# A mixed shared and routed FFN: the combination of a pair of tiles divided over two places of VectorE's step, and the first rows and last stores moved

## The chip, the cores and the metric

The kernel runs on one core of a Trainium2 chip. The metric is the device time of one execution in microseconds; the median of the runs is compared. The engines are TensorE (PE: matmul and transpose through the array), VectorE (DVE), ScalarE (ACT), GpSimd (POOL) and SyncE (SP), which here issues nearly all transfers. Each engine runs its own instruction stream in order, and they meet only through semaphores.

## What is computed

x is [4, 1024, 512] in float32: 4096 rows, 32 tiles of 128 rows. The reference is one modulated block: a time mix and channel mix, then a feed-forward with one shared and eight routed experts. Only the last part touches the change:

```
x = x + ga * attn(layernorm(x) * (1 + ca) + sa)
h = layernorm(x) * (1 + cb) + sb
shared = silu(h @ Wsg.T) * (h @ Wsu.T) @ Wsd.T                 # 704 wide
routed = sum over the two best experts of  w_e * (silu(h @ Wg_e.T) * (h @ Wu_e.T)) @ Wd_e.T   # 352 wide
x = x + gb * (routed + shared)
```

Products are made in three matmuls each: every float32 factor is split into a rounded high part and the remainder (names ending in _hi and _lo), and high x high, high x low and low x high are summed.

## The kernel before

The kernel has stages. After the time mix and the channel mix (stages one and two, up to about 900 us) come three sweeps over the feed-forward: EARLY (tiles 0 to 15 through the shared expert), ROUTED (39 expert tiles of 256 rows, 78 units of 128) and LATE (tiles 16 to 31 through the shared expert). The shared expert is 704 wide and is done as two halves of 352; one (tile, half) is a unit, and its work is the same as that of a routed unit.

A unit is a fixed chain. TensorE makes the up products into PS_G and PS_U (24 matmuls of 352 columns, lines 449 to 451), ScalarE makes silu (L1060), VectorE multiplies into hid (L1537), TensorE turns hid (L1815), ScalarE copies the high part out (hid_hi, L1053), VectorE subtracts for hid_lo (L1541), and TensorE makes the down product (nine matmuls of 512 columns, L1839 to L1841). The two halves of a tile add up in one bank, PS_Y. After half 1 VectorE gates the bank by mod3 and adds it to the residual rows in `base` (base_of, L1549 and L1554). TensorE works one unit ahead: in a step it turns hid of the unit before, makes the up product of this unit, then the down product of the unit before. The order within a step is written by hand, in `late_step` of each engine (L771 for SP, L1143 for ScalarE, L1634 for VectorE, L1887 for TensorE), and `sweep_part` unrolls the first and last steps around a hardware loop. t counts tiles: LATE's steps run from 15 to 32.

```
# TensorE, one late step (L1893 to L1899)
if t.back(-1).real(): turn_shared(LATE, t.back(-1))
for half in range(2):
    turn_hid(*before); up(LATE, t, half); down(*before)
```

`down` of half 0 also waits until VectorE has gated the previous tile's bank (L1829).

Beside the units, the late sweep combines the routed results. GpSimd gathers, for each pair of tiles q, the rows of the best and the second best expert (cb_y1, cb_y2, L908). ScalarE makes cb_out = w1 * cb_y1 (`first_product`, L1130 to L1141); VectorE adds w2 * cb_y2 (L1623, 'both'), multiplies by the gate (L1628, 'gated') and adds `base` (L1631, 'out'); SP stores the pair's 512 KB (`store_out`, L765). One pair is combined in each step: q = t - 17 on ScalarE and VectorE (steps 17 to 32), q = t - 18 on SP. ScalarE does first_product(q) and VectorE combine(q) at the very end of the step, after both halves. The buffers cb_y1, cb_y2 and cb_out have two slots, and lie in the two raw buffers that held unsplit weights before. The profile calls all three raw.

SP's lines that are touched: `load_late_rows` (L740) loads the 128 rows of a late tile into ex_x once the slot's former rows are turned; `load_shared_again` (L748) loads one half of the shared weights (2 MB) once the raw buffer is free; `routed_step` (L754) calls the latter in its last two steps, and the first late rows are loaded only after both, by the late sweep (L771). The wait at the end (L780) is for all stores.

Of the kernel before, what the change touches and what calls it, by code (L numbers as in the profile page):

```python
# [12 lines left out]
ALU = mybir.AluOpType  # L13
# [6 lines left out]
P = 128  # L20
D = 512
C = D // P
B, T = 4, 1024
N = B * T
NT = N // P
TPB = T // P
# [7 lines left out]
NJ = (2 * N + E * (R - 1)) // R  # L34
NU = NJ * R // P
SPLIT = NT // 2
# [78 lines left out]
LATE = Part(SPLIT, NT, NU, NU, ROUTED)  # L115
# [32 lines left out]
def build(nc, io, out):  # L148
    x_d = io["x"].rearrange("b t d -> (b t) d")
    out_d = out.rearrange("b t d -> (b t) d")  # L150
# [9 lines left out]
    h3_d = scratch("h3_rows", [N, D])  # L160
# [4 lines left out]
    with ctx:  # L165
# [143 lines left out]
        base = sb("base", [P, NT, D])  # L309
# [5 lines left out]
        w2 = sb("w2", [P, NT, 1])  # L315
# [211 lines left out]
        def _(sp):  # L527
# [209 lines left out]
                    sp.wait_ge(*x_pe.done(SPLIT + 2 * t.n + half - 2, "turned"))  # L737
                    sp.dma_start(ex_x[:, half, :], xs_d[bass.ds(row_of, P), :]).then_inc(ex_in[half], 16)

            def load_late_rows(t):  # L740
                row_of = sp.snap(t.n * P) if t.pair is not None else t.n * P
                sp.wait_ge(*x_pe.done(t.n + NU - 2, "turned"))
                sp.dma_start(ex_x[:, t.p, :], h3_d[bass.ds(row_of, P), :]).then_inc(sx_in[t.p], 16)

            for k in range(SC):
                sp.wait_ge(sc_out[k], 32 * len(range(k, NT, SC)))

            def load_shared_again(i):  # L748

                t = Tile(None, NJ + i, NJ + 2)  # L750
                sp.wait_ge(*rw_lo_vec.done(t.n - 2, "dn_lo"))
                load_raw(sp, t.p, io["sh_gu"][i], io["sh_dn"][i])

            def routed_step(t):  # L754
                if t.back(-1).real():
                    load_rows(t.back(-1))
                if t.real() and t.back(-2).real():
                    load_expert(t.back(-2))
                if t.pair is None and t.n in (NJ - 2, NJ - 1):
                    load_shared_again(t.n - (NJ - 2))  # L760

            sweep(sp, NJ, 2, 0, routed_step)
# [7 lines left out]

            def late_step(t):  # L771
                if t.back(-2).real():
                    load_late_rows(t.back(-2))
                    load_residual(t.back(-2))
                q = t.pairs_since(SPLIT + 2)
                if q.real():
                    store_out(q)

            sweep_part(sp, LATE, 2, 2, late_step)
            for p in range(2):  # L780
                sp.wait_ge(final_out[p], 16 * (NT // 4))
            sp.wait_ge(zero_out, 16 * NT)


# [129 lines left out]
        def _(act):  # L914
# [167 lines left out]
            def store_y(t, half):  # L1082
                row_of = act.snap((2 * t.n + half) * P) if t.pair is not None else (2 * t.n + half) * P
                act.wait_ge(*y_row_vec.done(2 * t.n + half, "y"))
                act.dma_start(ys_d[bass.ds(row_of, P), :], y_rows[:, half, :]).then_inc(ys_out[half], 16)
# [44 lines left out]
            def first_product(t):  # L1130

                if t.back(2).real():
                    act.wait_ge(final_out[t.p], 16 * t.half)
                else:
                    act.wait_ge(*rw_lo_vec.done(NJ + 1, "dn_lo"))
                act.wait_ge(y1_in[t.p], 32 * t.half + 32)
                act.activation(act_col[:, t.p:t.p + 1], eps[:], ACT.Copy)
                for a in range(2):
                    last = act.activation(cb_out[:, t.p, a, :], cb_y1[:, t.p, a, :], ACT.Copy,
                                          scale=w1[:, bass.ds(2 * t.n + a, 1), :].rearrange("p a b -> p (a b)"))  # L1140
                last.then_inc(cb_act.sem, 1)  # L1141

            def late_step(t):  # L1143
                q = t.pairs_since(SPLIT + 1)
                if t.real():
                    if t.back(-1).real():
                        shared_x_hi(LATE, t.back(-1))
                    for half in range(2):
                        if t.only(SPLIT):
                            expert_hi(Tile(None, NJ + 1, NJ + 2), half)  # L1150
                        hidhi(*LATE.before(t, half))
                        silu(LATE, t, half)
                        if t.only(SPLIT):
                            store_y(ROUTED.last(), half)
                elif t.only(NT):
                    hidhi(LATE, LATE.last(), 1)
                if q.real():
                    first_product(q)

            sweep_part(act, LATE, 1, 1, late_step)  # L1160

# [2 lines left out]
        def _(dve):  # L1164
# [374 lines left out]
            def hidlo(part, t, half):  # L1539
                dve.wait_ge(*u_act.done(part.unit(t, half), "hid_hi"))  # L1540
                dve.tensor_tensor(flat(hid_lo[:]), PS_H[:, 0:FK * P], flat(hid_hi[:]).bitcast(F32),  # L1541
                                  ALU.subtract).then_inc(u_vec.sem_of["hid_lo"], 1)
# [72 lines left out]
            sweep_part(dve, ROUTED, 1, 1, routed_step)  # L1615


            def combine(t):
                batch = t.n // (TPB // 2)
                dve.wait_ge(y2_in[t.p], 32 * t.half + 32)  # L1620
                dve.wait_ge(*cb_act.done(t.n, "first"))
                for a in range(2):
                    last = dve.scalar_tensor_tensor(cb_out[:, t.p, a, :], cb_y2[:, t.p, a, :],  # L1623
                                                    w2[:, bass.ds(2 * t.n + a, 1), :].rearrange("p a b -> p (a b)"),
                                                    cb_out[:, t.p, a, :], ALU.mult, ALU.add)
                last.then_inc(cb_vec.sem, 1)
                dve.wait_ge(*cb_vec.done(t.n, "both"))
                dve.tensor_tensor(cb_out[:, t.p], cb_out[:, t.p], mod3[:, bass.ds(batch, 1), :].to_broadcast([P, 2, D]),  # L1628
                                  ALU.mult).then_inc(cb_vec.sem, 1)
                dve.wait_ge(*cb_vec.done(t.n, "gated"))  # L1630
                dve.tensor_tensor(cb_out[:, t.p], cb_out[:, t.p], base[:, bass.ds(2 * t.n, 2), :],  # L1631
                                  ALU.add).then_inc(cb_vec.sem, 1)

            def late_step(t):  # L1634
                q = t.pairs_since(SPLIT + 1)
                if t.real():
                    if t.back(-1).real():
                        x_lo(t.back(-1).p, t.back(-1).n + NU)
                    for half in range(2):
                        before = LATE.before(t, half)  # L1640
                        hidlo(*before)
                        hid_of(LATE, t, half)
                        if t.only(SPLIT):
                            expert_lo(Tile(None, NJ + 1, NJ + 2), half)
                        if before[0] is ROUTED:
                            y_of_unit(*before[1:])
                        elif not half:
                            base_of(LATE, t.back(1))
                elif t.only(NT):
                    hidlo(LATE, LATE.last(), 1)  # L1650
                    base_of(LATE, LATE.last())
                if q.real():
                    combine(q)

            sweep_part(dve, LATE, 1, 1, late_step)

# [284 lines left out]
```

## Time and profile before

| what | us |
|---|---|
| median of 3 runs | 1899.61 (1895.79 to 1904.87) |
| profiled execution | 1899.84 |
| its span, first to last instruction | 1898.1 |
| late sweep, from its first turn to the last store | about 1647 to 1898 |

| engine | busy us | share |
|---|---|---|
| TensorE | 1753.4 | 92% |
| VectorE | 1331.3 | 70% |
| ScalarE | 722.7 | 38% |
| GpSimd | 567.6 | 30% |

A span is what lies between the first and the last instruction; the execution's time has 1.7 us around it. In the timeline a row is one instruction (or several alike), with its start, its duration, and in brackets the idle time of the engine just before it and what ended that. In the chain that ended last a row says how much a piece adds to it, which for overlapping matmuls is less than their duration. The granted clock is a share of TensorE's full 2.4 GHz; at 0.5 it is 1.2.

### The profile page before, as it was taken

What the parts mean: (1) busy time and instruction counts of PE and PEld (TensorE: products, weight loads), DVE (VectorE), ACT (ScalarE), POOL (GpSimd) and SP (SyncE); (2) the same over time, 40 slices, a digit from 0 to 9 for tenths busy, and PEclk for the clock granted to TensorE, in tenths of its full rate; (3) what the DMA queues carried; (4) which work ended last, traced back from release to release, by engine and by line L of the source; (5) the groups of instructions that cost most, each with busy time, mean ns of one, the idle gap of its engine ahead of it and who ended that gap; (6) DMA issues with size and microseconds to landing.
All of it is one profiled execution on the core that took longest, in us unless ns stands there. A gap on an engine that the chain in (4) does not pass through costs nothing.

```text
span 1898.1 us, 30073 instructions
## 1 busy us (share of the span) xinstructions
PE 1753.4 (92%) x9188; PEld 1520.5 (80%) x9188; DVE 1331.3 (70%) x2365; ACT 722.7 (38%) x1150; POOL 567.6 (30%) x659
## 2 busy tenths in 40 slices
PE   4599999997888999987899999999999999999997
PEld 0488888885777777776889989999999999888886
DVE  4899999983899888896733246666666666655555
ACT  2344444442444343343211135454545454422222
POOL 0343333322577667664125500000000000033432
PEclk8699999999998888897999999999999999999998
DMA  8333334334844433433167626767676767645442
GB/s 331 102 116 120 120 120 120 120 98 135 304 148 135 149 136 134 140 99 103 56 233 257 232 69 221 249 230 252 227 255 225 250 234 244 222 141 159 139 159 89
DMA packets 143262, 326.23 MB, mean 172 GB/s; under 512 B 20280, under 2 KB 20280, under 8 KB 137712
## 3 DMA queue, kind: packets, MB, share of 16 engines
q1 hardware_dynamic: 121744, 271.65, 42.9%
q0 software_dynamic: 10240, 33.56, 5.4%
q10 hardware_dynamic: 11232, 20.45, 2.8%
q8 instruction: 23, 0.38, 0.1%
q14 instruction: 23, 0.19, 0.0%
HBM read 217.56 MB, written 108.05 MB: 172 GB/s over the span
## 4 chain that ended last, share of the span: by engine, by line
PE 70%; DVE 18%; issue 5%; DMA 3%; ACT 2%; another core or an unknown queue 1%; DVEq 1%; POOL 1%; SPq 0%; ACTq 0%; POOLq 0%
PE bank L449 17%; PE bank L451 16%; PE bank L450 16%; DVE mix L1340 5%; PE bank L1839 5%; PE bank L1841 4%; PE bank L1840 4%; PE bank L460 4%; PE bank L1815 2%; DVE xh L1325 2%; DVE raw L1628 1%; DMA ex_x<-h_rows 1%; DMA stage<-in_w_k 1%; DVE h_lo L1395 1%; DVE raw L1623 1%
## 5 line engine op out<-in xcount | busy, mean ns | idle before, releaser
L449 PE MATMUL bank<-gu_hi,ex_x_hi 128*128 128x352 f32 x1136 | 382.4, 337 | 2.3 <-DVE gu_lo L1560 1.5
L451 PE MATMUL bank<-gu_hi,ex_x_lo 128*128 128x352 f32 x1136 | 369.6, 325 | 0.0
L450 PE MATMUL bank<-gu_lo,ex_x_hi 128*128 128x352 f32 x1136 | 369.4, 325 | 0.0
L908 POOL DMA_INDIRECT raw<-expert_out_rows,slots x64 | 78.7, 1229 | 702.6 <-DVE dn_lo L1560 582.5
L1537 DVE TENSOR_TENSOR hid<-bank,sg_t 128x352 f32<-128x352 f32 x142 | 74.5, 524 | 280.3 <-ACT sg_t L1060 259.4
L1060 ACT ACTIVATE sg_t<-bank 128x352 f32<-128x352 f32 x142 | 65.9, 464 | 401.0 <-PE bank L451 367.4
L449 PEld LDWEIGHTS bank<-gu_hi,ex_x_hi 128*128 128x128 f32 x1136 | 216.2, 190 | 2.9 <-DVE gu_lo L1560 1.8
L450 PEld LDWEIGHTS bank<-gu_lo,ex_x_hi 128*128 128x128 f32 x1136 | 216.3, 190 | 0.0
L451 PEld LDWEIGHTS bank<-gu_hi,ex_x_lo 128*128 128x128 f32 x1136 | 215.5, 190 | 0.0
L1839 PE MATMUL bank<-dn_hi,hid_hi 128*128 128x512 f32 x426 | 170.4, 400 | 12.9 <-DVE hid_lo L1541 12.8
L1841 PE MATMUL bank<-dn_hi,hid_lo 128*128 128x512 f32 x426 | 168.5, 396 | 0.0
L1840 PE MATMUL bank<-dn_lo,hid_hi 128*128 128x512 f32 x426 | 166.7, 391 | 0.0
L1560 DVE TENSOR_TENSOR gu_lo<-raw,gu_hi 128x2816 fp32r<-128x2816 f32 x41 | 126.4, 3083 | 1.4 <-ACT gu_hi L1077 1.4
L449 PE MATMUL bank<-w_r_hi,xm_hi 128*128 128x512 f32 x256 | 103.6, 405 | 14.4 <-DVE h1T L1268 10.0
L1416 DVE TENSOR_TENSOR ex_x_lo<-bank,ex_x_hi 128x512 fp32r<-128x512 f32 x110 | 75.5, 686 | 51.1 <-ACT ex_x_hi L1068 23.8
L1077 ACT ACTIVATE gu_hi<-raw 128x2816 fp32r<-128x2816 f32 x41 | 105.0, 2562 | 13.0 <-issue 12.6
L1340 DVE SCALAR_TENSOR_TENSOR mix<-diff,vecs,h2T 128x128 f32<-128x128 f32 x256 | 107.6, 487 | 1.6 <-POOL diff L847 1.6
L449 PE MATMUL bank<-w_k_hi,xm_hi 128*128 128x512 f32 x256 | 106.0, 414 | 0.0
L1277 DVE SCALAR_TENSOR_TENSOR stage<-diff,vecs,h1T 128x128 f32<-128x128 f32 x384 | 102.7, 338 | 2.6 <-POOL diff L815 2.6
L1839 PEld LDWEIGHTS bank<-dn_hi,hid_hi 128*128 128x128 f32 x426 | 80.4, 189 | 29.8 <-DVE hid_lo L1541 16.9
L450 PE MATMUL bank<-w_r_lo,xm_hi 128*128 128x512 f32 x256 | 102.5, 400 | 0.0
L451 PE MATMUL bank<-w_r_hi,xm_lo 128*128 128x512 f32 x256 | 102.3, 400 | 0.0
(213 smaller groups left out, 3997.3 us busy)
## 6 DMA issues: line engine op xcount, KB each, us to landing
raw<-in_ex_gu SPq DMA_DIRECT2D x39, 1408.0 KB, 6.5
expert_in_rows<-zero_rows SPq DMA_DIRECT2D x32, 624.0 KB
raw<-in_ex_dn SPq DMA_DIRECT2D x39, 512.0 KB, 7.4
ex_x<-expert_in_rows SPq DMA_DIRECT2D x78, 256.0 KB, 2.8
expert_out_rows<-y_rows ACTq DMA_DIRECT2D x78, 256.0 KB, 2.1
h_rows<-h_t SPq DMA_DIRECT2D x64, 256.0 KB, 2.5
x_t<-in_x SPq DMA_DIRECT2D x32, 256.0 KB, 2.8
timemix_rows<-o_t SPq DMA_DIRECT2D x32, 256.0 KB, 2.0
```

What stands on the lines that cost most here:

```text
L449: pe.matmul(acc, act_hi[i], w_hi[i], start=(i == 0), stop=False)
L450: pe.matmul(acc, act_hi[i], w_lo[i], start=False, stop=False)
L451: last = pe.matmul(acc, act_lo[i], w_hi[i], start=False, stop=(i == chunks - 1))
L460: last = pe.transpose(bank[:, c * P:(c + 1) * P], rows[:, c * P:(c + 1) * P], ident[:])
L908: pool.indirect_dma_start(rows[:, pair % 2, a, :], None, ys_d, bass.IndirectOffsetOnAxis(ap=slots[:, k, n:n + 1], axis=0)).then_inc(arrive ...
L1077: act.activation(flat_of(gu_hi, t), raw[t.p][:, 0:C * GU], ACT.Copy).then_inc(rw_hi_act.sem, 1)
L1277: last = dve.scalar_tensor_tensor(mix1[:, m, c, :], diff1[:, c, :], vecs[:, mu, c:c + 1], h1T[:, t.p, c, 0:P], ALU.mult, ALU.add)
L1340: last = dve.scalar_tensor_tensor(mix2[:, m, c, :], diff2[:, c, :], vecs[:, mu, c:c + 1], h2T[:, t.p, c, 0:P], ALU.mult, ALU.add)
L1560: dve.tensor_tensor(flat_of(w_lo, t), raw[t.p][:, cols], flat_of(w_hi, t).bitcast(F32), ALU.subtract).then_inc(rw_lo_vec.sem, 1)
L1839: pe.matmul(PS_Y[:], hid_hi[:, c, :], dn_hi[w][:, c, :], start=start and c == 0, stop=False)
L1840: pe.matmul(PS_Y[:], hid_hi[:, c, :], dn_lo[w][:, c, :], start=False, stop=False)
L1841: last = pe.matmul(PS_Y[:], hid_lo[:, c, :], dn_hi[w][:, c, :], start=False, stop=stop and c == FK - 1)
```

## The change

VectorE's `combine` is divided. `both_rows(q)` (the addition of the second expert's rows) is called in half 0 of the step, behind hid_of; `gated_rows(q)` (gate and base) in half 1, ahead of hid_of. The pair is still q = t - 17. ScalarE's `first_product(q)` stays at the end of step t, and the last pair's is issued at the end of step 31 instead of in step 32. In step 32 the last pair is combined with base rows of tile 31 that hold only the residual, and a new function, `last_rows`, gates the last tile's bank and adds it straight into the output rows. SP stores the last pair as two tiles, each on its own. SP also loads the rows of the first late tile ahead of the second half of the shared weights.

```
--- before.py
+++ after.py
@@ -737,19 +737,19 @@
                     sp.wait_ge(*x_pe.done(SPLIT + 2 * t.n + half - 2, "turned"))
                     sp.dma_start(ex_x[:, half, :], xs_d[bass.ds(row_of, P), :]).then_inc(ex_in[half], 16)
 
+            for k in range(SC):
+                sp.wait_ge(sc_out[k], 32 * len(range(k, NT, SC)))
+
+            def load_shared_again(i):
+
+                t = Tile(None, NJ + i, NJ + 2)
+                sp.wait_ge(*rw_lo_vec.done(t.n - 2, "dn_lo"))
+                load_raw(sp, t.p, io["sh_gu"][i], io["sh_dn"][i])
+
             def load_late_rows(t):
                 row_of = sp.snap(t.n * P) if t.pair is not None else t.n * P
                 sp.wait_ge(*x_pe.done(t.n + NU - 2, "turned"))
                 sp.dma_start(ex_x[:, t.p, :], h3_d[bass.ds(row_of, P), :]).then_inc(sx_in[t.p], 16)
-
-            for k in range(SC):
-                sp.wait_ge(sc_out[k], 32 * len(range(k, NT, SC)))
-
-            def load_shared_again(i):
-
-                t = Tile(None, NJ + i, NJ + 2)
-                sp.wait_ge(*rw_lo_vec.done(t.n - 2, "dn_lo"))
-                load_raw(sp, t.p, io["sh_gu"][i], io["sh_dn"][i])
 
             def routed_step(t):
                 if t.back(-1).real():
@@ -757,6 +757,8 @@
                 if t.real() and t.back(-2).real():
                     load_expert(t.back(-2))
                 if t.pair is None and t.n in (NJ - 2, NJ - 1):
+                    if t.n == NJ - 1:
+                        load_late_rows(LATE.tile(SPLIT))
                     load_shared_again(t.n - (NJ - 2))
 
             sweep(sp, NJ, 2, 0, routed_step)
@@ -770,15 +772,21 @@
 
             def late_step(t):
                 if t.back(-2).real():
-                    load_late_rows(t.back(-2))
+                    if not t.back(-2).only(SPLIT):
+                        load_late_rows(t.back(-2))
                     load_residual(t.back(-2))
                 q = t.pairs_since(SPLIT + 2)
-                if q.real():
+                if q.real() and not q.only(NT // 2 - 1):
                     store_out(q)
 
             sweep_part(sp, LATE, 2, 2, late_step)
-            for p in range(2):
-                sp.wait_ge(final_out[p], 16 * (NT // 4))
+            last = NT // 2 - 1
+            sp.wait_ge(*cb_vec.done(last, "out"))
+            sp.dma_start(out_d[(NT - 2) * P:(NT - 1) * P, :], cb_out[:, last % 2, 0, :]).then_inc(final_out[0], 16)
+            sp.wait_ge(*base_vec.done(NT - 1, "base"))
+            sp.dma_start(out_d[(NT - 1) * P:NT * P, :], cb_out[:, last % 2, 1, :]).then_inc(final_out[1], 16)
+            sp.wait_ge(final_out[0], 16 * (NT // 4) + 16)
+            sp.wait_ge(final_out[1], 16 * (NT // 4))
             sp.wait_ge(zero_out, 16 * NT)
 
 
@@ -1152,10 +1160,12 @@
                         silu(LATE, t, half)
                         if t.only(SPLIT):
                             store_y(ROUTED.last(), half)
+                    if q.real():
+                        first_product(q)
+                    if t.only(NT - 1):
+                        first_product(q.back(-1))
                 elif t.only(NT):
                     hidhi(LATE, LATE.last(), 1)
-                if q.real():
-                    first_product(q)
 
             sweep_part(act, LATE, 1, 1, late_step)
 
@@ -1615,21 +1625,32 @@
             sweep_part(dve, ROUTED, 1, 1, routed_step)
 
 
-            def combine(t):
-                batch = t.n // (TPB // 2)
-                dve.wait_ge(y2_in[t.p], 32 * t.half + 32)
-                dve.wait_ge(*cb_act.done(t.n, "first"))
+            def both_rows(q):
+                dve.wait_ge(y2_in[q.p], 32 * q.half + 32)
+                dve.wait_ge(*cb_act.done(q.n, "first"))
                 for a in range(2):
-                    last = dve.scalar_tensor_tensor(cb_out[:, t.p, a, :], cb_y2[:, t.p, a, :],
-                                                    w2[:, bass.ds(2 * t.n + a, 1), :].rearrange("p a b -> p (a b)"),
-                                                    cb_out[:, t.p, a, :], ALU.mult, ALU.add)
+                    last = dve.scalar_tensor_tensor(cb_out[:, q.p, a, :], cb_y2[:, q.p, a, :],
+                                                    w2[:, bass.ds(2 * q.n + a, 1), :].rearrange("p a b -> p (a b)"),
+                                                    cb_out[:, q.p, a, :], ALU.mult, ALU.add)
                 last.then_inc(cb_vec.sem, 1)
-                dve.wait_ge(*cb_vec.done(t.n, "both"))
-                dve.tensor_tensor(cb_out[:, t.p], cb_out[:, t.p], mod3[:, bass.ds(batch, 1), :].to_broadcast([P, 2, D]),
+
+            def gated_rows(q):
+                batch = q.n // (TPB // 2)
+                dve.wait_ge(*cb_vec.done(q.n, "both"))
+                dve.tensor_tensor(cb_out[:, q.p], cb_out[:, q.p], mod3[:, bass.ds(batch, 1), :].to_broadcast([P, 2, D]),
                                   ALU.mult).then_inc(cb_vec.sem, 1)
-                dve.wait_ge(*cb_vec.done(t.n, "gated"))
-                dve.tensor_tensor(cb_out[:, t.p], cb_out[:, t.p], base[:, bass.ds(2 * t.n, 2), :],
+                dve.wait_ge(*cb_vec.done(q.n, "gated"))
+                dve.tensor_tensor(cb_out[:, q.p], cb_out[:, q.p], base[:, bass.ds(2 * q.n, 2), :],
                                   ALU.add).then_inc(cb_vec.sem, 1)
+
+            def last_rows(t):
+                dve.wait_ge(*u_pe.done(LATE.unit(t, 1), "down"))
+                dve.wait_ge(*base_vec.done(t.n - 1, "base"))
+                dve.tensor_tensor(gated_t[:], PS_Y[:], mod3[:, B - 1, :], ALU.mult).then_inc(base_vec.sem, 1)
+                rows = cb_out[:, (t.n // 2) % 2, 1, :]
+                dve.wait_ge(*cb_vec.done(t.n // 2, "out"))
+                dve.wait_ge(*base_vec.done(t.n, "gated"))
+                dve.tensor_tensor(rows, rows, gated_t[:], ALU.add).then_inc(base_vec.sem, 1)
 
             def late_step(t):
                 q = t.pairs_since(SPLIT + 1)
@@ -1639,7 +1660,11 @@
                     for half in range(2):
                         before = LATE.before(t, half)
                         hidlo(*before)
+                        if half and q.real():
+                            gated_rows(q)
                         hid_of(LATE, t, half)
+                        if not half and q.real():
+                            both_rows(q)
                         if t.only(SPLIT):
                             expert_lo(Tile(None, NJ + 1, NJ + 2), half)
                         if before[0] is ROUTED:
@@ -1648,9 +1673,10 @@
                             base_of(LATE, t.back(1))
                 elif t.only(NT):
                     hidlo(LATE, LATE.last(), 1)
-                    base_of(LATE, LATE.last())
-                if q.real():
-                    combine(q)
+                    both_rows(q)
+                    dve.wait_ge(sr_in[LATE.last().p], 16 * (NT // 2))
+                    gated_rows(q)
+                    last_rows(LATE.last())
 
             sweep_part(dve, LATE, 1, 1, late_step)
 
```

## Rows read from the trace of the kernel before

**Rows 1.** The page's first part: busy time, share of the span, instructions.
```profile
PE 1753.4 (92%) x9188; PEld 1520.5 (80%) x9188; DVE 1331.3 (70%) x2365; ACT 722.7 (38%) x1150; POOL 567.6 (30%) x659
```

**Rows 2.** Waits of TensorE, 1560 to 1899 us: total us, times, longest us.
```profile
PE bank L1839 <- DVE hid_lo L1541: 12.4, 15, 4.0
PE bank L460 <- DMA ex_x<-h_rows: 3.2, 1, 3.2
```

**Rows 3.** Timeline of step t = 18: start, duration (us), engine, line, operation.
```profile
1699.90 0.39 PE L1839 MATMUL bank<-dn_hi,hid_hi 128*128 128x512 f32 x1
...
1700.16 0.46 ACT L1060 ACTIVATE sg_t<-bank 128x352 f32<-128x352 f32 x1 [3.39 <-PE bank L451]
...
1700.61 1.33 ACT L1139 ACTIVATE raw<-raw,w 128x512 f32<-128x512 f32 x2
...
1702.04 1.41 DVE L1623 SCALAR_TENSOR_TENSOR raw<-raw,w 128x512 f32<-128x512 f32 x2 [0.79 <-ACT raw L1139]
...
1703.49 1.23 DVE L1628 TENSOR_TENSOR raw<-raw,mod 128x1024 f32<-128x1024 f32 x1
...
1704.75 1.22 DVE L1631 TENSOR_TENSOR raw<-raw,base 128x1024 f32<-128x1024 f32 x1
...
1706.49 0.55 DVE L1541 TENSOR_TENSOR hid_lo<-bank,hid_hi 128x384 fp32r<-128x384 f32 x1
...
1707.09 0.50 PE L1839 MATMUL bank<-dn_hi,hid_hi 128*128 128x512 f32 x1 [0.35 <-DVE hid_lo L1541]
...
1709.47 0.69 DVE L1549 TENSOR_TENSOR gated_t<-bank,mod 128x512 f32<-128x512 f32 x1 [1.54 <-PE bank L1841]
...
1710.26 0.69 DVE L1554 TENSOR_TENSOR base<-base,gated_t 128x512 f32<-128x512 f32 x1
...
1710.87 0.55 DVE L1541 TENSOR_TENSOR hid_lo<-bank,hid_hi 128x384 fp32r<-128x384 f32 x1
```

**Rows 4.** Timeline of VectorE: two routed steps; first and last combination within steps.
```profile
1619.01 0.52 DVE L1537 TENSOR_TENSOR hid<-bank,sg_t 128x352 f32<-128x352 f32 x1 [1.97 <-ACT sg_t L1060]
...
1632.42 0.53 DVE L1537 TENSOR_TENSOR hid<-bank,sg_t 128x352 f32<-128x352 f32 x1 [2.29 <-ACT sg_t L1060]
...
1688.45 1.42 DVE L1623 SCALAR_TENSOR_TENSOR raw<-raw,w 128x512 f32<-128x512 f32 x2 [0.80 <-ACT raw L1139]
...
1880.78 1.41 DVE L1623 SCALAR_TENSOR_TENSOR raw<-raw,w 128x512 f32<-128x512 f32 x2 [0.78 <-ACT raw L1139]
```

**Rows 5.** The chain that ended last: start, us that the piece adds.
```profile
1633.97 0.44 PE bank L460 x4
...
1707.09 0.50 PE bank L1839
...
1707.83 0.23 PE bank L1841
...
1885.23 0.79 PE bank L1839
...
1886.45 0.43 PE bank L1841
```

**Rows 6.** Timeline around the first late tile: SP, VectorE and TensorE.
```profile
1642.74 0.62 SPq L743 DMA_DIRECT2D ex_x<-h_rows  x1
...
1645.97 0.53 DVE L1537 TENSOR_TENSOR hid<-bank,sg_t 128x352 f32<-128x352 f32 x1 [2.31 <-ACT sg_t L1060]
...
1650.57 0.63 PE L460 MATMUL bank<-ident,ex_x 128*128 128x128 f32 x4 [3.18 <-DMA ex_x<-h_rows]
...
1657.62 0.53 DVE L1537 TENSOR_TENSOR hid<-bank,sg_t 128x352 f32<-128x352 f32 x1 [4.54 <-ACT sg_t L1060]
```

**Rows 7.** Stretches: length, PE busy, granted clock, DMA share, GB/s.
```profile
1651.00:1657.00 6.00, 6.00 (x30) 0.72 0.49 160
1700.00:1750.00 50.00, 48.02 (x276) 43.62 (x275) 29.43 (x41) 14.37 (x31) 19.17 (x16) 1.00 0.46 142
1882.00:1889.00 7.00, 3.77 (x9) 0.60 0.19 75
```

**Rows 8.** Timeline of VectorE's tail, and SP's last wait.
```profile
1889.48 0.69 DVE L1549 TENSOR_TENSOR gated_t<-bank,mod 128x512 f32<-128x512 f32 x1 [4.30 <-PE bank L1841]
...
1893.58 1.23 DVE L1631 TENSOR_TENSOR raw<-raw,base 128x1024 f32<-128x1024 f32 x1
...
SPq L782 <- DMA out<-raw: 2.4, 1, 2.4
```

More of the change, by code:

```diff
@@ L738, in load_rows @@
                     sp.dma_start(ex_x[:, half, :], xs_d[bass.ds(row_of, P), :]).then_inc(ex_in[half], 16)
[L740 to L743, printed above, removed]
             for k in range(SC):
@@ L752, in load_shared_again, with load_late_rows @@
                 load_raw(sp, t.p, io["sh_gu"][i], io["sh_dn"][i])
+            def load_late_rows(t):
+                row_of = sp.snap(t.n * P) if t.pair is not None else t.n * P
+                sp.wait_ge(*x_pe.done(t.n + NU - 2, "turned"))
+                sp.dma_start(ex_x[:, t.p, :], h3_d[bass.ds(row_of, P), :]).then_inc(sx_in[t.p], 16)
             def routed_step(t):
```

## The prediction

> **What bounds the kernel now.** I read the page first: TensorE is busy for 92% of the span [rows 1], so whatever lengthens TensorE's row of work lengthens the kernel, and the other engines count only where TensorE waits for them. Then the waits of TensorE from 1560 us on, the stretch that the change touches [rows 2]. There are two kinds. The down product of L1839 waited 15 times for hid_lo, 12.4 us in total, 4.0 us in the longest. And the turning of the first late tile waited once, 3.2 us, for its rows out of memory.
>
> Then one step of the late sweep in order of time [rows 3], t = 18. TensorE starts the down product of half 0 at 1699.90, with no wait, straight after the second up product. Beside it ScalarE makes the second silu (1700.16) and the pair's first product (1700.61), and VectorE then does the whole combination (1702.04, 1703.49, 1704.75). The next hid_lo stands behind that block on VectorE (1706.49), so the down product of the next step starts only at 1707.09. That is the wait which the division is aimed at.
>
> What it costs follows from periods. Two routed units take 1632.42 - 1619.01 = 13.41 us and turn two tiles; a late step has the same products but turns one, at 0.44 us each [rows 4, 5]. Its floor is 12.97 us, and 12.53 for t = 31, which turns none. The combinations of t = 17 and t = 31 start 1880.78 - 1688.45 = 192.33 us apart [rows 4]; 13 x 12.97 + 12.53 is 181.14. So 11.2 us is what these 14 steps lose, refills of the array included.
>
> **The change, part by part.**
>
> *VectorE's division.* both_rows(q) goes to half 0, behind hid_of(t, 0); gated_rows(q) goes to half 1, ahead of hid_of(t, 1). The pair q = t - 17 is the same on both engines, and ScalarE still issues first_product(q) behind silu(t, 1), at the end of step t. So both_rows(q) waits at half 0 for a product that ScalarE makes only once TensorE has done the up product of half 1. VectorE works in order. Queued behind this wait are base_of(t - 1) and hidlo(t, 0), and TensorE's down(t, 0) waits for both. Today that down product waits for nothing [rows 3].
>
> The new gap in TensorE, counted from where down(t, 0) starts today: to the start of both_rows 1702.04 - 1699.90 = 2.14; both_rows 1703.49 - 1702.04 = 1.45; base_of 0.79 + 0.61, from the starts at 1709.47, 1710.26 and 1710.87; from hid_lo's start to the down product 1707.09 - 1706.49 = 0.60 [rows 3]. That is 5.59 us. The first matmul after a wait takes 0.50 us of the chain and the others 0.23 [rows 5], so 0.27 more: 5.86 us in each step t = 17 to 31. The two gating operations (1.26 from start to start, then 1.22) now run beside the down product, so hid of half 1 ends about 8.5 us after the old start; the next turn would be ready at 5.86 + 2.07 + 0.44 = 8.4, so 0.2 us of wait stays at full clock and none at half.
>
> *TensorE's clock.* The granted clock was 0.72 in the stretch behind the 3.2 us wait and 0.60 around the 4.0 us wait, and 1.00 from 1700 to 1750; the full level is 2.4 GHz and the lower one 1.2 [rows 7]. Waits of 5.6 us are longer than either. At the lower level a down matmul takes 0.43 of the chain for 0.23 [rows 5]: nine of them 1.8 us. The front wait together with its slow stretch cost 1657.62 - 1645.97 - 6.71 = 4.94 us (6.71 is half of 13.41), 1.7 more than the wait [rows 2, 4, 6]. I take 1.6 per step, a little less, since part of the slow stretch can fall into the wait itself. 0 is the low end; 2.3 the high one, should turn and up product behind it be slow too.
>
> The Trainium skill, "TensorE: Matmul & The Clock Gate", section "HAM oscillation — how this bites in real kernels", describes just this pattern, a burst that starts at the lower clock after every wait, and its example pays 26.7 us of penalty over 32 bursts, 0.83 each. By that figure the estimate for this kernel would be 1978 us, 11 lower than mine; the rows of this trace are nearer to 1.7, and the sum goes by them.
>
> *ScalarE.* first_product(15) moves from t = 32 to t = 31. It lies in the new wait of TensorE; the next hid_hi needs the down product to end first. Nothing. Were that cover gone it would put 1.3 us ahead of hid_hi.
>
> *The tail.* Today 14.03 us pass from the start of the combination of t = 31 (1880.78) to the end of VectorE's last operation (1893.58 + 1.23) [rows 4, 8]. After: down(31, 0) starts 3.45 behind both_rows(14) and at the lower clock takes 0.79 + 8 x 0.43 = 4.2; turn, hid_hi and hid_lo's start 1.1; the last down product starts 0.6 later and takes 4.25 (1889.48 - 1885.23) [rows 3, 5, 8], ending at 13.6. both_rows(15) and gated_rows(15) (about 4 us) lie beside it. last_rows adds two operations of 128x512, 0.79 + 0.69: 15.1, or 1.1 us more than today. The trace shows no store of 256 KB at the end; the wait for today's last store of 512 KB took 2.4 us [rows 8]. With half the bytes it is not longer, and at best the two microseconds go: I take 0. The added wait on sr_in is for rows asked for many steps earlier. The divided store also lets tile 30 go earlier; only the last one counts.
>
> *SP.* load_late_rows(16) goes ahead of the second shared weights. It waits for the turn of the last routed tile's first half, which starts at 1633.97 [rows 5], where today it is issued at 1642.74 behind the weights, and wanted by TensorE about 1647.4 [rows 6]. The weights wait for dn_lo anyhow, so nothing queued behind is delayed. All of the 4.94 us goes; 0 is the other bound. The rows of tile 17 stay behind the weights; they are needed a unit later. The last pair leaves SP's sweep and costs nothing there.
>
> **The sum.** Profiled execution 1899.84 us (the median of the runs shown is 1899.61). The 14 steps: 181.14 + 14 x (5.86 + 1.6) - 192.33 = +93.2. Front -4.9, tail +1.1. In all +89.4, so 1989 us.
>
> **The rivals.**
>
> *The wait without the clock.* 14 x 6.06 for the steps gives +73.6, and with front and tail some +69.5: 1969 us. For it: the other 14 waits of L1839, 8.4 us or 0.6 each [rows 2], kept the full clock. Against it: both waits over 3 us lost it.
>
> *The lower clock lasts longer.* With 2.3 us per step, +99: 1999 us; with half an up product behind it slow as well (some 3.4 per step), +114: 2014 us. For it: the stretch at 0.60 outlasted the last down product. Against it: behind the front wait the clock came back within one up product.
>
> *The division works, and the kernel is faster.* This needs ScalarE's product to be there before VectorE reaches both_rows, a product issued one step ahead. Then hid_lo is nowhere behind the block: -11.2; front -4.9; and with the 4.0 us wait gone the last operation ends 9.2 us behind the old start of down(31, 0) (2.1 down product, 1.1 to hid_lo, 0.6, then 4.0 for both_rows and gated_rows, 1.5 for last_rows) in place of 2.14 + 14.03 = 16.2: -7.0. In all -23: 1877 us. It decides from the point at which both_rows no longer finds ScalarE behind it. For it: the aim, and that the product's inputs are gathered early. Against it: the position of first_product in the code, and 2.14 us from the down product's start to the product's end even today.
>
> *The change doesn't do what it says for the front:* the rows of tile 16 land late still, because the first shared weights fill the queues. +5 us on any of these.
>
> **How the numbers follow.** Forecast 1989 us: 0.66. The wait at full clock: 0.12. A longer slow clock: 0.15. The division works: 0.05. Another course near no change, a wait that mostly hides: 0.02. The range takes in the full-clock case and the slow clock at 2.3: 1965 to 2004 us, somewhat over 8 in 10. About 0.5%, 9.5 us, is what a measurement of this kernel can tell from no change. Faster 0.05, same 0.02, slower 0.93.
>
> **What the profile after would show.** Among TensorE's waits, L1839 behind hid_lo with 15 waits of about 5.6 us; on VectorE the scalar-tensor-tensor of both_rows with 15 idle times of over 5 us, released by ScalarE's product; late steps of about 20.4 us; a granted clock under 1 through the late sweep; no wait for the first late tile. TensorE's busy time would rise by the slow matmuls alone. The prediction is wrong if late steps stay at 13 us, if the idle time before both_rows is short, or if the granted clock stays at 1.00 with waits over 5 us (then 1969).

## The result, and the profile after

| | before | changed |
|---|---|---|
| median of 6 runs, us | 1899.31 | 1987.64 |
| profiled execution, us | 1899.84 | 1982.2 |
| its span, us | 1898.1 | 1980.4 |
| mean granted clock over the span | 0.957 | 0.938 |

The changed kernel takes 1.046 of the time of the kernel before, with a 95% interval of 1.0439 to 1.0481: slower by 88 us. The forecast was 1989 us.

The first part of the page, and the waits of TensorE and of VectorE from 1560 us on (total us, times, longest us), in the changed kernel:

```profile
PE 1775.1 (90%) x9188; PEld 1535.4 (78%) x9188; DVE 1328.7 (67%) x2365; ACT 722.4 (36%) x1150; POOL 556.7 (28%) x659
```

```profile
PE bank L1865 <- DVE hid_lo L1551: 84.0, 16, 6.8
PE bank L449 <- DVE gu_lo L1570: 1.5, 1, 1.5
...
DVE raw L1632 <- ACT raw L1147: 108.3, 15, 8.5
```

VectorE's wait at the same place in the kernel before:

```profile
DVE raw L1623 <- ACT raw L1139: 13.1, 15, 0.9
```

Lines have moved: the down product is L1865 (it was L1839), hid_lo L1551, both_rows L1632, gated_rows L1640 and L1643, ScalarE's product L1147. Against [rows 2] the waits for hid_lo have grown from 12.4 to 84.0 us at almost the same number, and the wait for the first late rows is gone. VectorE's wait is what has changed most. It stands 15 times, 7.2 us on average, before both_rows, and each time ScalarE's product ends it. In the kernel before it stood there 15 times too, but for 0.9 us each. TensorE is busy for 21.7 us more with the same 9188 matmuls: matmuls at the lower clock.

One step of the late sweep in the changed kernel, in order of time:

```profile
1751.18 0.53 DVE L1547 TENSOR_TENSOR hid<-bank,sg_t 128x352 f32<-128x352 f32 x1 [2.90 <-ACT sg_t L1068]
1758.89 1.41 DVE L1632 SCALAR_TENSOR_TENSOR raw<-raw,w 128x512 f32<-128x512 f32 x2 [7.18 <-ACT raw L1147]
1760.22 0.68 DVE L1559 TENSOR_TENSOR gated_t<-bank,mod 128x512 f32<-128x512 f32 x1
1761.05 0.69 DVE L1564 TENSOR_TENSOR base<-base,gated_t 128x512 f32 x1
1761.65 0.55 DVE L1551 TENSOR_TENSOR hid_lo<-bank,hid_hi 128x384 fp32r<-128x384 f32 x1
1762.12 1.22 DVE L1640 TENSOR_TENSOR raw<-raw,mod 128x1024 f32<-128x1024 f32 x1
1763.48 1.23 DVE L1643 TENSOR_TENSOR raw<-raw,base 128x1024 f32<-128x1024 f32 x1
1764.62 0.52 DVE L1547 TENSOR_TENSOR hid<-bank,sg_t 128x352 f32<-128x352 f32 x1
...
1779.42 1.41 DVE L1632 SCALAR_TENSOR_TENSOR raw<-raw,w 128x512 f32<-128x512 f32 x2 [7.17 <-ACT raw L1147]
```

VectorE finishes hid of half 0 at 1751.7 and then does nothing until 1758.89. Only then come base_of and hid_lo, for which TensorE's down product waits. The next both_rows starts 20.53 us later; in the kernel before a step took 13.8.

TensorE's wait in one of the later steps:

```profile
1946.72 0.77 PE L1865 MATMUL bank<-dn_hi,hid_hi 128*128 128x512 f32 x1 [5.41 <-DVE hid_lo L1551]
```

The chain that ended last, from the end of the step before to behind the hid_lo of 1761.65 (start, us added), and TensorE over the sweep (length, busy, granted clock, DMA share, GB/s):

```profile
1745.55 0.43 PE bank L1867
1745.98 0.48 PE bank L460 x4
...
1746.79 0.16 PE bank L449
...
1761.65 0.56 DVE hid_lo L1551
...
1762.35 0.77 PE bank L1865
1763.12 0.43 PE bank L1866
```

```profile
1700.00:1960.00 260.00, 194.65 (x977) 0.83 0.32 98
```

The down matmuls behind the wait add 0.43 us each, where they add 0.23 at full clock [rows 5]. Over the whole sweep the granted clock is 0.83, where it was 1.00 before (from 1700 to 1750 in [rows 7], and to 1879 in the same trace). Nine down matmuls are slow each time; with the up product behind them (1746.79) the clock is at 2.4 GHz again.

**Where the 82.3 us between the two spans lie.** The same marks in both traces, the changed kernel's first as rows of VectorE's timeline:

```profile
1638.10 0.53 DVE L1547 TENSOR_TENSOR hid<-bank,sg_t 128x352 f32<-128x352 f32 x1 [2.31 <-ACT sg_t L1068]
...
1644.80 0.53 DVE L1547 TENSOR_TENSOR hid<-bank,sg_t 128x352 f32<-128x352 f32 x1 [1.52 <-ACT sg_t L1068]
...
1675.62 1.42 DVE L1632 SCALAR_TENSOR_TENSOR raw<-raw,w 128x512 f32<-128x512 f32 x2 [8.50 <-ACT raw L1147]
...
1963.31 1.42 DVE L1632 SCALAR_TENSOR_TENSOR raw<-raw,w 128x512 f32<-128x512 f32 x2 [7.03 <-ACT raw L1147]
...
1977.25 0.69 DVE L1653 TENSOR_TENSOR raw<-raw,gated_t 128x512 f32<-128x512 f32 x1
```

| stretch | before, us | changed, us | difference |
|---|---|---|---|
| to the hid of the last routed tile's half 0 | 1645.97 | 1638.10 | -7.9 |
| from it to the next hid (the front edit) | 11.65 | 6.70 | -4.95 |
| to the first both_rows | 30.83 | 30.82 | 0.0 |
| to the both_rows of t = 31 (14 steps) | 192.33 | 287.69 | +95.4 |
| to the end of VectorE's last operation | 14.03 | 14.63 | +0.6 |
| to the end of the span | 3.29 | 2.46 | -0.8 |

The first row is no part of the change, which touches nothing so early; executions differ there by some microseconds (in other traces the same hid stands at 1639.02 and at 1637.08). Without it the change costs 90.2 us in this profile. The very last down product (t = 31, half 1) waits only 1.23 us, and its first matmul takes 0.50 us where the one at 1946.72 took 0.77:

```profile
1972.68 0.50 PE L1865 MATMUL bank<-dn_hi,hid_hi 128*128 128x512 f32 x1 [1.23 <-DVE hid_lo L1551]
```

### The profile page after: what moved, and what is told of

Same layout as the page of the kernel before. It is cut to its first block, busy times and chain, and to the rows that moved or that the text cites. A ratio compares the mean times of both kernels' runs of the same rounds, so it can differ in the third digit from the quotient of the medians.

```text
span 1980.4 us, 30075 instructions
## 1 busy us (share of the span) xinstructions
PE 1775.1 (90%) x9188; PEld 1535.4 (78%) x9188; DVE 1328.7 (67%) x2365; ACT 722.4 (36%) x1150; POOL 556.7 (28%) x659
## 4 chain that ended last, share of the span: by engine, by line
PE 74%; DVE 15%; issue 4%; ACT 2%; DMA 2%; POOL 1%; another core or an unknown queue 1%; DVEq 1%; SPq 0%; ACTq 0%; POOLq 0%
PE bank L449 17%; PE bank L451 17%; PE bank L450 17%; PE bank L1865 6%; PE bank L1867 5%; PE bank L1866 5%; DVE mix L1350 5%; PE bank L460 4%; PE bank L1841 2%; DVE xh L1335 2%; DVE h_lo L1405 1%; DMA stage<-in_w_k 1%; PE bank L1784 1%; DVE raw L1632 1%; ACT raw L1147 1%
## 5 line engine op out<-in xcount | busy, mean ns | idle before, releaser
L916 POOL DMA_INDIRECT raw<-expert_out_rows,slots x64 | 67.7, 1058 | 796.2 <-DVE dn_lo L1570 577.5
L1865 PE MATMUL bank<-dn_hi,hid_hi 128*128 128x512 f32 x426 | 180.7, 424 | 84.5 <-DVE hid_lo L1551 84.4
L1867 PE MATMUL bank<-dn_hi,hid_lo 128*128 128x512 f32 x426 | 178.2, 418 | 0.0
L1866 PE MATMUL bank<-dn_lo,hid_hi 128*128 128x512 f32 x426 | 176.6, 415 | 0.0
L1865 PEld LDWEIGHTS bank<-dn_hi,hid_hi 128*128 128x128 f32 x426 | 85.8, 201 | 102.8 <-DVE base L1564 86.7
L1867 PEld LDWEIGHTS bank<-dn_hi,hid_lo 128*128 128x128 f32 x426 | 86.3, 203 | 21.0
```

Of the source, the lines that this page charges most:

```text
L1865: pe.matmul(PS_Y[:], hid_hi[:, c, :], dn_hi[w][:, c, :], start=start and c == 0, stop=False)
L1866: pe.matmul(PS_Y[:], hid_hi[:, c, :], dn_lo[w][:, c, :], start=False, stop=False)
L1867: last = pe.matmul(PS_Y[:], hid_lo[:, c, :], dn_hi[w][:, c, :], start=False, stop=stop and c == FK - 1)
```

## The experiments

Two theories at the start. A: VectorE waits at half 0 for a product that ScalarE makes only at the end of the step; everything behind it on VectorE is late, and TensorE's clock falls in addition. B: the division itself costs, since part of the block now stands ahead of hid_lo. Ratios are to the kernel before on the same chip, whose median there was 1886 to 1892 us.

**1. ScalarE's product between the halves** (e1_product_mid), in the changed kernel:

```diff
                         silu(LATE, t, half)
+                        if not half and q.real():
+                            first_product(q)
                         if t.only(SPLIT):
                             store_y(ROUTED.last(), half)
-                    if q.real():
-                        first_product(q)
```

> Theory A (VectorE waits at half 0 for a product that ScalarE makes only at the end of the step): with ScalarE's first_product(q) moved between the halves, behind silu(t, 0), the product takes 2.0 us from the end of the up product while TensorE's down product and turn take 2.4, so it is hidden, and both_rows waits under 1 us. Late steps of 12.97 us, no wait of L1865 over 1 us inside the sweep, granted clock 1.00 from 1700 us on, and 1877 us (ratio to before about 0.988). Rival B (the division itself costs, because a part of the combination now stands ahead of hid_lo of half 0): the steps stay well over 13.8 us and the time stays above the kernel before.

Measured: ratio 0.9874 (0.9843 to 0.9905). TensorE's waits from 1500 us on:

```profile
PE bank L1865 <- DVE hid_lo L1551: 2.2, 2, 1.2
PE bank L449 <- DVE gu_lo L1570: 1.5, 1, 1.5
```

and VectorE around one both_rows, with the neighbour a step later:

```profile
1824.17 1.41 DVE L1632 SCALAR_TENSOR_TENSOR raw<-raw,w 128x512 f32<-128x512 f32 x2 [0.90 <-ACT raw L1147]
...
1837.18 1.42 DVE L1632 SCALAR_TENSOR_TENSOR raw<-raw,w 128x512 f32<-128x512 f32 x2 [0.80 <-ACT raw L1147]
```

The division is kept, half 0 and half 1 are as in the changed kernel on VectorE, and 12.95 to 13.01 us remain per step; the 14 steps take 181.11 us (1668.69 to 1849.80), where the floor worked out in the prediction was 181.14. That they agree to 0.03 us is partly luck, since the first both_rows started late, behind its gathered rows and not behind the product:

```profile
1668.69 1.44 DVE L1632 SCALAR_TENSOR_TENSOR raw<-raw,w 128x512 f32<-128x512 f32 x2 [2.58 <-DMA raw<-expert_out_rows,slots]
```

One wait in ScalarE's order makes the whole difference between 1.046 and 0.987. Theory B falls. It is also a version that beats both kernels.

**2. The combination whole again, the rest of the change kept** (e2_undivided):

```diff
                     for half in range(2):
                         ...
-                        if half and q.real():
-                            gated_rows(q)
                         hid_of(LATE, t, half)
-                        if not half and q.real():
-                            both_rows(q)
                         ...
+                    if q.real():
+                        both_rows(q)
+                        gated_rows(q)
```

> The whole combination back at the end of the step, with the other parts of the change (rows of the first late tile ahead, last pair gated on its own, product of the last pair in step 31, a store per tile) kept. Theory A: the slowdown goes with the placing of both_rows alone; steps of 13.8 us again, front -4.9 us, tail about -3.8 us on VectorE and -0.8 on the last store: 1890 us, ratio 0.995. Rival C (the early rows, the divided store or the moved product disturb the late sweep): clearly slower than before.

Measured: 0.995 (0.9931 to 0.9968). The other parts are a gain of their own, and the slowdown goes with the placing. The waits for hid_lo are those of [rows 2] again:

```profile
PE bank L1864 <- DVE hid_lo L1551: 11.5, 15, 4.1
```

**3. The front edit alone** (e3_front), on the kernel before: load_late_rows of the first late tile called ahead of load_shared_again(1), and nowhere else (its definition moves up with it, not shown here).

```diff
                 if t.pair is None and t.n in (NJ - 2, NJ - 1):
+                    if t.n == NJ - 1:
+                        load_late_rows(LATE.tile(SPLIT))
                     load_shared_again(t.n - (NJ - 2))
...
-                    load_late_rows(t.back(-2))
+                    if not t.back(-2).only(SPLIT):
+                        load_late_rows(t.back(-2))
```

> The kernel before with nothing but the rows of the first late tile asked for ahead of the second half of the shared weights. Expected: the wait of 3.2 us and its slow stretch vanish, 6.7 us between the two hid operations where 11.65 passed, -4.9 us: 1894.5 us, ratio 0.9975. Rival: the rows still land late, or the later weights make a new wait of the same size: 1899.

Measured: 0.9971 (0.9953 to 0.9989). The two hid operations stand 6.70 us apart (1639.02 and 1645.72 in its trace), the wait for the rows is gone, and no other has come.

**4. The wait filled with useless matmuls** (e4_filler), in the changed kernel. They write a bank that nobody reads, so no result depends on them:

```diff
                     up(LATE, t, half)
+                    if half and t.pairs_since(SPLIT + 1).real():
+                        for _ in range(22):
+                            pe.matmul(PS_RT[:], dn_hi[0][:, 0, 0:P], dn_hi[0][:, 0, :], start=True, stop=True)
                     down(*before)
```

> The changed kernel with 22 matmuls of 512 columns (useless ones, into a bank that nobody reads) ahead of the down product of half 0 in steps 17 to 31, where TensorE now waits. They take 22 x 0.22 = 4.8 us, less than the wait of 5.4, so they lie in it. If the granted clock is what makes a step 20.48 and not 18.6 to 18.9: the granted clock stays at 1.00, the step falls to about 18.9 (12.97 + 5.6 + a little, by the wait of hid), 15 x 1.6 = 24 us, to about 1964 us. If the slow stretches cost nothing beside other work, or the waits themselves are the whole loss: the time stays at 1988 or rises.

Measured: 1.0359 (1.0326 to 1.0392).

**5. The changed kernel again** (e0_changed_again), without an edit:

> The changed kernel itself, unaltered, on this chip, so that e4_filler has a neighbour measured against the same kernel before. Expected ratio 1.046 as measured first, against 1.036 of e4_filler: 19 us for the granted clock. If this chip's ratio is 1.036 too, the filler bought nothing.

Measured: 1.045 (1.0426 to 1.0474); its steps in the hardware loop were 20.4 to 20.6 us once more. One step with the filler, TensorE and then VectorE, and the granted clock:

```profile
1726.18 5.16 PE L1927 MATMUL bank<-dn_hi 128*128 128x512 f32 x22
1731.86 0.47 PE L1865 MATMUL bank<-dn_hi,hid_hi 128*128 128x512 f32 x1 [0.52 <-DVE hid_lo L1551]
```

```profile
1728.33 1.48 DVE L1632 SCALAR_TENSOR_TENSOR raw<-raw,w 128x512 f32<-128x512 f32 x2 [7.22 <-ACT raw L1147]
```

```profile
1700.00:1750.00 50.00, 49.00 (x261) 1.00 0.31 93
```

TensorE is given about 5 us more to do in each step, and the kernel is faster by about 1% (1.045 to 1.036, some 17 us, where 24 had been expected; by the two traces the 14 steps are 21.4 us shorter, 265.33 against 286.68). VectorE's wait is as long as before, 7.2 us; what has changed is that the down product behind it runs at the full clock. The steps are 18.97 us on average (1728.33 to 1937.02 for eleven of them is 18.97) against 20.48: the clock is 1.5 us of a step's loss, and 6.0 is the wait.

**6. The combination whole, in half 1** (e5_undivided_half1), on the kernel of experiment 1: both_rows and gated_rows together where gated_rows stood.

```diff
                         if half and q.real():
+                            both_rows(q)
                             gated_rows(q)
                         hid_of(LATE, t, half)
-                        if not half and q.real():
-                            both_rows(q)
```

> ScalarE's product between the halves as in e1_product_mid, and the whole combination undivided in the place of gated_rows (half 1, behind hid_lo, ahead of hid of half 1). Theory A says that what counts is where the product is made and that the block stands behind hid_lo, not that it is divided: VectorE's block of 3.9 us ends about 8 us after the up product of half 0, hid of half 1 by 8.5, while TensorE needs it at 8.8. So no wait, steps of 12.97 to 13.2 us, and the time of e1_product_mid within 3 us (ratio 0.987 to 0.989). Theory D (the division is needed): waits of the turn behind hid of half 1 of 1 us or more a step, +14 us or more against e1_product_mid.

Measured: 0.9892 (0.9862 to 0.9921). The intervals overlap with those of experiment 1, so the time doesn't separate them; the trace does. The loop steps were 13.40 us, not 12.97 to 13.2:

```profile
PE bank L1840 <- DVE hid L1547: 2.2, 11, 0.3
```

The turn waits 0.2 us for hid of half 1, 11 times. The 14 steps took 185.80 us (1668.79 to 1854.59), 4.7 more than in experiment 1. I had put the end of the block too early: base_of waits 1.3 us for the down product before it, which both_rows filled in experiment 1. Against that, both_rows has another place in the step here; from the hid of the last routed tile's half 0 to the end of the span it is 231.7 us against 228.4, 3.3 more. So once the product is early, dividing is worth 3 to 5 us, seen in one trace of each. Of the 24 us that experiment 1 gains on the kernel before, some 9 belong to the other parts (experiment 2), and some 10 are left for the early product and a place of the block behind hid_lo.

**7. The combination whole, in half 0** (e7_undivided_half0), likewise, where both_rows stood.

```diff
-                        if half and q.real():
-                            gated_rows(q)
                         hid_of(LATE, t, half)
                         if not half and q.real():
                             both_rows(q)
+                            gated_rows(q)
```

> ScalarE's product between the halves, and the whole combination undivided in the place of both_rows (half 0, ahead of base_of and of hid_lo). By the rows of e1_product_mid, hid_lo then starts 2.4 us later, 7.2 us after the end of the up product, where TensorE wants it done at 6.3: a wait of about 1.5 us in each of 15 steps and 0.27 of refill, no fall of the granted clock, steps of 14.7 us: some 25 us above e1_product_mid, ratio about 1.001. If division is without effect here too: the time of e1_product_mid.

Measured: 1.0122 (1.0102 to 1.0143), well beyond the 1.001 expected. The waits were sized right, their effect was not. TensorE's timeline has waits of 1.6 us in steps that were 14.9 us long, and of 2.0 us in steps of mostly 16.8:

```profile
1705.33 0.47 PE L1864 MATMUL bank<-dn_hi,hid_hi 128*128 128x512 f32 x1 [1.66 <-DVE hid_lo L1551]
...
1754.16 0.47 PE L1864 MATMUL bank<-dn_hi,hid_hi 128*128 128x512 f32 x1 [1.99 <-DVE hid_lo L1551]
```

```profile
1699.00:1714.00 15.00, 13.34 (x79) 1.00 0.46 141
...
1748.00:1765.00 17.00, 15.01 (x80) 0.90 0.41 123
```

**8. The same with a filler of 7 matmuls** (e9_filler7), to tell the clock from anything else in the loop:

```diff
+                    if half and t.pairs_since(SPLIT + 1).real():
+                        for _ in range(7):
+                            pe.matmul(PS_RT[:], dn_hi[0][:, 0, 0:P], dn_hi[0][:, 0, :], start=True, stop=True)
                     down(*before)
```

> e7_undivided_half0 with 7 useless matmuls of 512 columns (1.6 us) in the wait of 1.6 to 2.0 us ahead of the down product of half 0. In e7 the steps whose wait was 1.65 us took 14.88 us at full clock, and those with 1.95 to 2.0 us took 16.8 with a granted clock of 0.90. If the clock is the 1.9 us between them: all steps 14.9 to 15.2, granted clock 1.00, 8 x 1.9 = 15 us less than e7, ratio about 1.004. If something else in the hardware loop makes those steps longer (register work, gathers): ratio 1.012 as before.

Measured: 1.0044 (1.0027 to 1.0061). All loop steps were 15.2 us (1737.47, 1752.65, 1767.83), and the clock stayed up:

```profile
1700.00:1850.00 150.00, 146.46 (x823) 1.00 0.43 133
```

So the clock was 15 of the 21 us by which experiment 7 missed its 1.001. The other 6 were a wrong size: the steps are 15.2 us at the full clock too, where 14.7 were expected, and in experiment 7 the first wait was 3.6 us long.

**9. The last pair's both_rows ahead of the last hid_lo** (e8_tail), on the kernel of experiment 1.

```diff
# ScalarE
                         if not half and q.real():
                             first_product(q)
+                            if t.only(NT - 1):
+                                first_product(q.back(-1))
...
-                    if t.only(NT - 1):
-                        first_product(q.back(-1))
# VectorE
+                    if t.only(NT - 1):
+                        both_rows(q.back(-1))
                 elif t.only(NT):
                     hidlo(LATE, LATE.last(), 1)
-                    both_rows(q)
```

> e1_product_mid with the last pair's product made in half 0 of step 31 and both_rows of the last pair ahead of the last hid_lo. In the tail of e1_product_mid VectorE works without a pause from the last hid_lo to its last operation, 5.9 us; 1.4 us of that is both_rows, now in an idle time of 1.3 us before it. Expected: 1.0 to 1.3 us off the end, too little for the timing to tell, to be read in the profile. If the last down product and not VectorE sets the end: nothing.

Measured: 0.9878 (0.986 to 0.9896), which the time can't tell from experiment 1. From the both_rows of t = 31 to the end of VectorE's last operation 13.25 us passed in experiment 1 and 11.89 here:

```profile
1846.36 1.41 DVE L1632 SCALAR_TENSOR_TENSOR raw<-raw,w 128x512 f32<-128x512 f32 x2 [0.79 <-ACT raw L1147]
...
1857.56 0.69 DVE L1653 TENSOR_TENSOR raw<-raw,gated_t 128x512 f32<-128x512 f32 x1
```

1.4 us, a little over what was expected; seen in one trace, not in the median.

**10. The division with the early product, and nothing else** (e10_division_alone), on the kernel before: combine in its two parts at the two places, first_product between the halves, and rows, last pair and stores as they were.

```diff
# ScalarE
                         silu(LATE, t, half)
+                        if not half and q.real():
+                            first_product(q)
...
                     hidhi(LATE, LATE.last(), 1)
-                if q.real():
                     first_product(q)
# VectorE
+                        if half and q.real():
+                            gated_rows(q)
                         hid_of(LATE, t, half)
+                        if not half and q.real():
+                            both_rows(q)
...
                     base_of(LATE, LATE.last())
-                if q.real():
-                    combine(q)
+                    both_rows(q)
+                    gated_rows(q)
```

> The kernel before with only the division of the combination and ScalarE's product between the halves; rows of the first late tile, last pair and stores as before. If the parts add up: steps 12.97, -11.2 us; the 3.2 us wait for the rows and its slow stretch stay; in the tail the wait of 4.0 us becomes 1.2 and the clock stays up, some -4 us; together 14 to 15 us, ratio 0.9922 to 0.9927. If the parts stand in each other's way, the ratio is at that of e1_product_mid (0.987) or at 0.995.

Measured: 0.9936 (0.9917 to 0.9955). The steps are 12.97 us on average (1683.41 to 1839.09 for 12 of them). The wait for the first late rows, kept here, was 4.2 us long in this trace. The parts add up within the intervals: 0.6% for the division together with the early product, 0.5% for the rest (experiment 2), 1.1 of the 1.3% of experiment 1. How the 0.6% is shared between the two is not shown: the early product was not run with the whole combination at its old place. The rows of the kernel before leave room for it, since VectorE stood 0.9 us for the product in each step and TensorE 0.6 us behind the block.

## Why the prediction was right, point by point

- **The new wait.** Right in place and in size. It was put together from durations of the trace before as 5.59 us and a refill of 0.27; with the clock kept up (experiment 4) a step lost 6.0. By the profile the wait is 5.4 us (5.41 in the row at 1946.72), since the last up matmul's modelled end reaches into it. Experiment 1 shows that it hangs on ScalarE's order alone.
- **The clock.** Taken as 1.6 us per step from two single waits; 1.5 by experiment 4. The step came out at 20.48 against 12.97 + 5.86 + 1.6 = 20.43. The Trainium skill, "TensorE: Matmul & The Clock Gate", section "HAM oscillation — how this bites in real kernels", has an example that pays 0.83 us per burst. The value measured here is nearly double, as the rows had said.
- **The 14 steps.** +93.2 forecast, +95.4 measured. Most of the rest, 1.6 us, lies in the first four intervals, which were 20.6 to 21.2 us where 20.43 was forecast.
- **The front.** -4.94 forecast, -4.95 measured, and experiment 3 has it as 0.3% of the time by itself.
- **The tail.** +1.1 forecast on VectorE, +0.6 measured, because the last down product ran at the full clock and VectorE's own row set the end; the prediction had it take 4.25 us, at the lower clock. The last store I took at no gain; at half the size it gave 0.8 us (from VectorE's last operation to the end of the span 3.3 us in experiments 3 and 10, which store 512 KB, and 2.5 in 1, 2 and 9, which store 256 KB). Both are small mis-sizings in the same direction.
- **The sum.** 1989 forecast, 1987.64 measured. The profiled execution was 1982.2, 7.9 us of which the stages ahead had gained by themselves, so the match of the median to 1.4 us is partly luck; the 90.2 us found in the trace against 89.4 is the fairer comparison.
- **The rivals.** Full clock in spite of the waits (1969): experiment 4 made that case real and came out at 1.036, which is 1967 on the first chip, but the clock had to be held up by hand. A longer slow stretch (1999): no; it was over by the next up product. The division works (1877, ratio 0.988): not in this kernel, and with one call moved exactly so (0.9874).

What was argued and not run: that ScalarE's move of the last product to step 31 costs nothing, and that the wait added on sr_in is never felt. No row shows either as a wait. Nor was the early product run without any other change, which bears on experiment 10 but not on the slowdown.

## What to carry to other kernels

When a block is divided and a part moved ahead in one engine's step, look where its inputs are produced in the other engines' steps, by position and not only by index: the same pair number on two engines says nothing about which half of the step it is made in. A part that waits is paid by everything queued behind it, here a 1.4 us operation that held a critical 0.55 us one for 5.4 us. Put the producer first (here one call, 1.3% faster than before in place of 4.6% slower), then ask whether the division is still needed.

## What was not expected of the hardware

- **Waits of 2.0 us already lose the clock, if not always.** In experiment 7 the ten loop steps had waits of 1.93 to 2.04 us; in eight of them the step was 16.7 to 16.8 us and TensorE ran at 1.2 GHz for a part of it, in two it was 15.2. The waits of 1.63 to 1.66 us there (TensorE's clock at 1.00), and one of 1.53 in the kernel before (1667.88), kept 2.4 GHz. A lost clock costs 1.6 us on top of a wait of 2.0: nearly a doubling of its price. In the two short steps the wait was 1.96 and 1.95 us, as long as in the others; what decided between them is not shown.
- **Useless work can pay.** 22 matmuls a step, about 5 us of TensorE's time, made the changed kernel about 1% faster, and 7 matmuls made experiment 7 0.8% faster (1.0122 to 1.0044).
- **The steps settle.** In both profiles of the changed kernel the later steps lie within 20.4 to 20.6 us, at 20.48 on average, whatever the first ones were (21.15 and 20.67). What sets that was not tried.
